# Solving only the diagonal blocks of 16 by substitution, and putting in the corner by two more matmul passes

## The chip, the cores and the metric

One core of a Trainium2 chip runs the kernel. It has a matmul engine (PE, TensorE), a vector engine (DVE), a scalar engine (ACT), GpSimd (POOL) and SyncE (SP), which issues DMAs. The metric is the device time of one execution in microseconds, the median of three runs.

## The reference

The kernel computes one "macaron" layer on x of 8 x 256 x 128: half a feed-forward part (FFN), an attention part, half the same FFN again. The FFN has ternary weights, a gated up projection and two hidden layers of 512. The attention part projects to q, k, v with short causal convolutions, and mixes five paths for each head (4 heads of 32): three FIR filters of v (3, 15 and 64 taps), v itself, and a delta rule by chunks of 32 tokens. A gate computed from x and from statistics of the five paths (mean, mean square, mean absolute value, norm) weighs them.

What the change touches is the delta rule. For each of 8 x 4 x 8 = 256 chunks:

```
attn = where(strict, -(kb @ k^T), 0)     # strictly lower, 32 x 32
T = inv(eye(32) - attn)                  # unit lower triangular
u = T @ v ;  w = T @ kb                  # both 32 x 32
# then over the 8 chunks of a sequence, one after the other:
local = where(incl, q @ k^T, 0)
u_i = u - w @ S ;  o = q @ S + local @ u_i ;  S = S + k^T @ u_i
```

## The kernel before

**Queues and order.** The five engines run their own instruction streams. All of them walk the same list, STEPS, written out by hand in `ffn_steps` and `att_steps`; each step is a kind, a part (0 and 1 the FFNs, 2 the attention) and an index. Engines wait for each other through semaphores, and each engine runs its own steps in the order of the list. PE writes to two rings of four PSUM banks: ring a is emptied by ACT, ring d by DVE; a step takes its banks by its position in the list. SP's queue has the loads of the FIR tiles and of the second FFN's weights, each behind a wait for a PE step.

**Layout.** The 8 sequences are handled in two halves of 4. Within a half, the 128 partitions are 4 sequences x 32 tokens of a chunk (or 4 heads x 32 channels), and for each head and chunk there is a 32 x 32 matrix in each partition block. Matmuls of the delta rule are 32 x 32 weights against 64 columns, four side by side on the array. An fp32 matmul has two records in the trace, and each has a weight load (PEld) beside it.

**The steps of the attention part**, in the order before:

- `qkv`, `sumsq`, `window`: projections with convolutions, norms, transposed windows of v for the FIR.
- `gram` (L851 on PE, L579 on ACT, L1172 on DVE): the products of k with kb and q, masked into `alt`, slot 0 the strict part (-attn), slot 1 the inclusive part.
- `lmat` (L1181): one DVE transpose puts the strict part (L) into the layout of the substitution: one chunk's matrix to a partition, its 32 x 32 elements along the free dimension; half 0's 128 matrices fill the 128 partitions.
- `solve` and, between the masks of the second gram, `substitute` (L1063 to L1074): for each column j of 31, `prod = L[j+1:, j] * T[j, 0:j+1]` and `T[j+1:, 0:j+1] -= prod`, two DVE instructions that depend on each other. Half 1's runs on GpSimd (L459, L461), after half 0's is done.
- `xt` (L1196): DVE transposes the inverse back, as weights for PE.
- `token` (L848): transposes of k, vb and kb to tokens in partitions. `fir` (L872): 16 FIR steps, in FIR_ORDER, the first eight for half 0; each needs its filter tile `toep`, of which two of four groups fit, so that groups are loaded again behind the steps that used them last (L390 to L392).
- `yy` (L884): `T @ [v, kb]`, 8 steps of 64 records. `aq` and `bo` (L894): products of w and u with k and q, 56 and 64 records a step. `first`, `rec`: the recurrence over chunks, a product on PE (L906), an addition (L1220) and a transpose (L1224) on DVE for each of 7 steps and half. `turn3`, `turn4`: the paths into the mixing layout.
- `sq`, `r1`, `r2`, `r3`: the statistics of the 10 path halves; a square on ACT (L502) and three DVE reduces (L1238, L1240, L1244). `turn`: their transpose for the gate.
- `gate` (L915, L917), `logit` (L924), `lturn`, `soft`, `prob`, `mul`, `addmix`, `add`, `rms`, `scale`, `wo`: gate, softmax, mixing, norm and output projection. Those of the first half are put between the steps of the second half's recurrence, those of the second half into the second FFN.

In the order before, half 0's substitution runs while PE does the tokens of both halves, the last eight windows and eight FIR steps. Then come yy, aq and bo of half 0, the recurrence of half 0 with four FIR steps and statistics beside it, yy, gates 0 and 1, aq, logits and bo of half 1, and the recurrence of half 1 with the mixing of half 0.

Of the kernel before, what the change touches and what calls it, by code (L numbers as in the profile page):

```python
# [24 lines left out]
SPLIT = 4  # L25
# [43 lines left out]
def att_steps():  # L69

    s = []
    for t in range(2):
# [23 lines left out]
    s += sums(9)
# [7 lines left out]
          "yy": 1, "bo": 1, "gate": 2, "logit": 1, "addmix": 1}  # L104
RING_D = {"mean": 1, "var": 1, "up": KT, "down": 1, "sumsq": 2, "gram": H, "aq": 1, "rec": 1,
# [30 lines left out]
STATS = ((4, 0), (0, 0), (1, 0), (2, 0), (4, 1), (3, 0), (0, 1), (1, 1), (2, 1), (3, 1))  # L136
# [10 lines left out]
         mtau=47, rt0=55, epsd=48)  # L147
# [6 lines left out]
          vk=0, bo=0, yu=4096, lmat0=32768, tinv0=33792, lmat1=6144, tinv1=7168, ssb=22016, alt=8192, vt0=24576, vt1=16384, aq1=19968, xt=14336, paths=24576,  # L154
          sq=36864, st=34816, stt=4096, hid=6144, hid0=16384, lg=18432, pl=4096, small=12288,
# [3 lines left out]
def program(nc, d, out):  # L159
    ctx = ExitStack()  # L160
    with ctx:
# [60 lines left out]
        sb("paths1", [128, AO["st"] - AO["paths"]], F32, c3)  # L222
# [15 lines left out]
        def ln_bufs(f):  # L238
            if f == 1:
# [124 lines left out]
        def _(e):  # L364
# [940 lines left out]
```

## Time and profile before

| what | us |
|---|---|
| median of three runs | 440.77 |
| lowest, highest | 439.73, 440.98 |
| profiled execution | 442.02 |
| its span | 440.3 |

The attention part takes the stretch from about 130 to 325 us. Every number in the rows further down is read from this one profiled execution. A row of a timeline merges like instructions that follow each other; "idle before" is the time in which the engine had nothing running, with what ended it, and "issue" there means that nothing in the profile accounts for it.

### The profile page before, as it was taken

How to read it: one execution, taken by the hardware profiler on the slowest of the kernel's cores; microseconds unless marked ns; L12 is line 12 of the kernel's file. 1: busy time of each engine (PE TensorE's matmuls, PEld its weight loads, DVE VectorE, ACT ScalarE, POOL GpSimd, SP SyncE). 2: the span in 40 equal slices, each digit the busy share in tenths (PEclk: the TensorE clock that was granted, in tenths of full speed). 3: DMA queues.
4: the chain of work that ended last, by engine and by line, in shares of the span. 5: the costliest groups of instructions: out<-in, count | busy, mean ns of one | idle time of the engine just before them, and what ended most of it. 6: DMA issues, size and time to landing. Idle time of an engine off the chain costs nothing.

```text
span 440.3 us, 9783 instructions
## 1 busy us (share of the span) xinstructions
PE 371.1 (84%) x4132; PEld 278.6 (63%) x4132; DVE 294.8 (67%) x461; ACT 277.7 (63%) x434; POOL 41.9 (10%) x103
## 2 busy tenths in 40 slices
PE   5599999999999998899488489366599687978996
PEld 3377776678866876799377376233267465556885
DVE  2796679628216845699696968667868696578433
ACT  4788956879677776383243265451576838558973
POOL 4000000000000100000788400000000000000000
PEclk9899999999999996889956889585999898989999
DMA  8900007400000000071600001600000000001001
GB/s 272 333 1 2 2 0 227 111 1 1 1 1 0 0 2 3 4 214 49 173 5 4 1 4 36 230 1 1 0 1 3 1 0 2 0 1 49 3 1 48
DMA packets 14325, 19.75 MB, mean 45 GB/s; under 512 B 960, under 2 KB 9152, under 8 KB 14272
## 3 DMA queue, kind: packets, MB, share of 16 engines
q1 hardware_dynamic: 14128, 18.94, 14.4%
q8 instruction: 44, 0.72, 0.6%
q14 instruction: 9, 0.07, 0.1%
q10 hardware_dynamic: 144, 0.01, 0.0%
HBM read 17.91 MB, written 1.05 MB: 43 GB/s over the span
## 4 chain that ended last, share of the span: by engine, by line
PE 58%; DVE 26%; issue 7%; ACT 7%; DMA 1%; DVEq 0%; SPq 0%; ACTq 0%
PE ps_a L723 11%; PE ps_a L724 11%; PE ps_a L827 8%; PE ps_a L894 2%; PE ps_a L884 2%; DVE arena L1074 2%; DVE arena L1071 2%; PE ps_d L794 2%; PE ps_d L858 2%; PE ps_a L917 2%; DVE acts L1121 2%; PE ps_d L724 2%; PE ps_d L723 2%; PE ps_d L894 2%; DVE hbuf L1116 2%
## 5 line engine op out<-in xcount | busy, mean ns | idle before, releaser
L723 PE MATMUL ps_a<-acts,w_f 128*128 128x512 f32 x256 | 103.6, 405 | 9.1 <-ACT acts L597 8.5
L724 PE MATMUL ps_a<-acts,w_f 128*128 128x512 f32 x256 | 101.7, 397 | 0.0
L723 PEld LDWEIGHTS ps_a<-acts,w_f 128*128 128x128 f32 x256 | 49.2, 192 | 22.6 <-ACT acts L597 10.2
L724 PEld LDWEIGHTS ps_a<-acts,w_f 128*128 128x128 f32 x256 | 49.2, 192 | 10.9 <-issue 0.7
L597 ACT ACTIVATE acts<-ps_a,vec 128x512 fp32r<-128x512 f32 x64 | 44.6, 697 | 0.0
L827 PE MATMUL ps_a<-xnp,conv_w 128*128 128x512 f32 x156 | 38.5, 404 | 0.0
L1140 DVE TENSOR_TENSOR acts<-gbuf,acts 128x512 fp32r<-128x512 f32 x32 | 21.6, 689 | 24.9 <-ACT acts L597 24.9
L1140 DVE TENSOR_TENSOR acts<-ghbuf,acts 128x512 fp32r<-128x512 f32 x32 | 21.2, 689 | 20.8 <-ACT acts L597 20.8
L827 PEld LDWEIGHTS ps_a<-xnp,conv_w 128*128 128x128 f32 x156 | 29.3, 188 | 8.2 <-issue 1.4
L987 DVE SCALAR_TENSOR_TENSOR arena<-ps_d,arena 128x512 f32<-128x512 f32 x16 | 11.0, 686 | 30.4 <-ACT arena L551 26.3
L594 ACT ACTIVATE gbuf<-ps_a,vec 128x512 f32<-128x512 f32 x32 | 22.3, 697 | 10.3 <-PE ps_a L724 10.2
L594 ACT ACTIVATE ghbuf<-ps_a,vec 128x512 f32<-128x512 f32 x32 | 22.4, 699 | 7.2 <-PE ps_a L724 7.1
L872 PE MATMUL ps_a<-toep,arena 96*32 96x96 f32 x512 | 23.8, 356 | 0.0
L906 PE MATMUL ps_d<-arena 32*32 32x64 f32 x448 | 11.6, 256 | 13.3 <-issue 6.7
L872 PEld LDWEIGHTS ps_a<-toep,arena 96*32 96x32 f32 x512 | 20.1, 130 | 3.1 <-issue 1.6
L723 PE MATMUL ps_a<-xn,w_f 128*128 128x512 f32 x32 | 15.3, 477 | 7.7 <-DVE ln L988 5.1
L906 PEld LDWEIGHTS ps_d<-arena 32*32 32x32 f32 x448 | 9.0, 129 | 19.2 <-issue 10.7
L502 ACT ACTIVATE arena<-arena 128x1024 f32<-128x1024 f32 x10 | 10.3, 1050 | 16.6 <-DVE arena L1227 16.3
L459 POOL TENSOR_TENSOR arena<-arena 128x31 f32<-128x31 f32 (+15 forms) x31 | 15.6, 503 | 46.9 <-DVE arena L1196 44.6
L642 ACT ACTIVATE arena<-ps_a 128x384 f32<-128x384 f32 x16 | 7.9, 491 | 17.1 <-PE ps_a L872 17.0
L884 PE MATMUL ps_a<-arena 32*32 32x64 f32 x512 | 10.2, 243 | 9.9 <-DVE arena L1196 5.3
L1116 DVE SCALAR_TENSOR_TENSOR hbuf<-ps_d,vec,gbuf 128x512 f32<-128x512 f32 x16 | 11.6, 748 | 8.4 <-ACT gbuf L567 5.2
(211 smaller groups left out, 778.5 us busy)
## 6 DMA issues: line engine op xcount, KB each, us to landing
toep<-in_fir SPq DMA_DIRECT2D x24, 288.0 KB, 6.5
w_in<-in_h SPq DMA_DIRECT2D x4, 1024.0 KB, 8.2
g_rows<-in_gW SPq DMA_DIRECT2D x4, 640.0 KB, 6.7
w_in<-in_w SPq DMA_DIRECT2D x6, 256.0 KB, 4.7
iobuf<-in_x SPq DMA_DIRECT2D x4, 256.0 KB, 6.5
toep<-in_taps SPq DMA_DIRECT2D x1, 768.0 KB, 6.7
y<-iobuf SPq DMA_DIRECT2D x3, 256.0 KB, 2.4
toep<-in_proj SPq DMA_DIRECT2D x1, 256.0 KB, 8.6
```

What stands on the lines that cost most here:

```text
L459: own(e.tensor_tensor(prod, lmat[1][:, j + 1:DH, j:j + 1].to_broadcast(shape), tinv[1][:, j:j + 1, 0:j + 1].to_broadcast(shape), ALU.mult))
L594: e.activation(gbuf[f][:, gi % 4], src[:, :], ACT.Gelu, scale=sc).then_inc(S["act_step"], 1)
L597: e.activation(acts[f][:, j % 3, 0, m], src[:, :], ACT.Gelu, scale=sc).then_inc(S["act_a"], 1)
L723: e.matmul(bank, w, hi, start=start, stop=False)
L724: return e.matmul(bank, w, lo, start=False, stop=stop)
L827: last = e.matmul(bank, conv_w[:, hw, ww], xnp[:, hx, 2 * i:2 * i + 2, o:o + L], start=n == 0, stop=n == len(todo) - 1)
L872: last = e.matmul(bank[32 * h:32 * h + 32, WIN * c4:WIN * c4 + WIN], vt[half][0:WIN, DH * h + 8 * grp + dl, :], toep[0:WIN, grp % 2, h, :, ...
L884: last = e.matmul(bank[r, 64 * n:64 * n + 64], xt[r, g, h, n], vk[r, g, h, n].rearrange("p x c -> p (x c)"), start=True, stop=True)
L894: last = e.matmul(bank[c, 64 * n:64 * n + 64], yu[r, g, h, n, o:o + DH], alt[g][r, h, n, 1:3].rearrange("p x c -> p (x c)"), start=True, s ...
L906: last = e.matmul(bank[r, 64 * b:64 * b + 64].rearrange("p (x t) -> p x t", x=2), s_sb[r, g, b], aqs[g][r, b, n], start=True, stop=True)
L1116: e.scalar_tensor_tensor(out=hbuf[f][:, m % 2], in0=ps_d[:, (dd + m) % NRING], scalar=vc("s2", m), in1=gbuf[f][:, (KT * j + m) % 4], op0=A ...
L1140: e.tensor_tensor(acts[f][:, j % 3, 1, m], gbuf[f][:, (KT * j + m) % 4], acts[f][:, j % 3, 0, m].bitcast(F32), ALU.subtract).then_inc(S["d ...
```

## The change

The unit lower matrix I - attn is split into its two diagonal blocks of 16 and the lower left 16 x 16 corner, called N here. The inverse D of the two diagonal blocks is found by substitution, for both blocks in one instruction, 15 steps instead of 31. The corner is put in by three passes on PE instead of one:

- `zz`: y = D [v, kb], evicted by ACT with a scale of 1 for the upper 16 tokens of a chunk and 0 for the lower (`top`);
- `ww`: N y, made with slot 0 of `alt`, where GpSimd has set the diagonal blocks' columns to zero (semaphore `cut`); DVE subtracts it from [v, kb] in place;
- `yy`: D ([v, kb] - N y), as before.

zz and ww have 8 steps each, of 64 records, as yy. GpSimd does half 1's blocks instead of the whole matrices, and begins when half 1's `lmat` is there. The steps are put in a new order. These are its core lines:

```
-    s += fir[0:4] + [("gram", 2, 1), ("lmat", 2, 1), ("solve", 2, 2), ("xt", 2, 0)]
-    s += [("token", 2, i) for i in (0, 1, 4, 5, 8, 9, 2, 3, 6, 7, 10, 11)]
-    s += [("window", 2, i) for i in range(8, 16)] + fir[4:12]
-    s += [("yy", 2, k) for k in range(4)] + [("turn4", 2, 0), ("turn4", 2, 1), ("sq", 2, 0), ("sq", 2, 1)] + sums(0)
...
+    s += fir[0:4] + [("solve", 2, 1), ("gram", 2, 1), ("lmat", 2, 1)]
+    s += [("token", 2, i) for i in (0, 1, 4, 5, 8, 9)] + [("zz", 2, k) for k in range(4)]
+    s += [("turn4", 2, 0)] + [("ww", 2, k) for k in range(4)] + [("turn4", 2, 1), ("r1", 2, 0), ("numbers", 2, 0)]
+    s += [("yy", 2, k) for k in range(4)] + [("token", 2, 10), ("token", 2, 11), ("r2", 2, 0)]
+    s += [("aq", 2, k) for k in range(4)] + [("bo", 2, k) for k in range(4)] + [("first", 2, 0)]
+    beside = {1: [("token", 2, 2), ("token", 2, 3)], 2: [("token", 2, 6), ("token", 2, 7), ("xt", 2, 1)],
+              3: [("window", 2, i) for i in range(8, 12)], 4: [("window", 2, i) for i in range(12, 16)] + [("sq", 2, 0)],
+              5: [fir[4], ("r3", 2, 0)], 6: [fir[5], ("sq", 2, 1), ("r1", 2, 1)], 7: [fir[6], ("r2", 2, 1)]}
     for n in range(1, NCH):
         s += [("rec", 2, n)] + beside[n]
+    s += [("turn3", 2, 0), fir[7], ("sq", 2, 2), ("r3", 2, 1)] + [("zz", 2, k) for k in range(4, 8)] + sums(2)
+    s += [("sq", 2, 3), ("ww", 2, 4), ("ww", 2, 5), ("ww", 2, 6), ("ww", 2, 7)] + [("yy", 2, k) for k in range(4, 8)] + sums(3)
+    s += [("sq", 2, 4)] + fir[8:10] + sums(4) + [("sq", 2, 5)] + [("bo", 2, k) for k in range(4, 8)] + sums(5) + fir[10:16]
+    s += [("turn", 2, 0)] + [("aq", 2, k) for k in range(4, 8)]
     half = [None] + [("rec", 2, NCH + n) for n in range(1, NCH)]
+    s += [("first", 2, 1), ("gate", 2, 0), ("sq", 2, 6), half[1], ("gate", 2, 1), ("r1", 2, 6), half[2], ("sq", 2, 7), ("r2", 2, 6),
+          ("logit", 2, 0), ("r3", 2, 6), half[3], ("logit", 2, 1)] + sums(7) + [("sq", 2, 8), ("lturn", 2, 0), ("soft", 2, 0)]
+    s += [half[4], ("round", 2, 0), ("r1", 2, 8), ("prob", 2, 0), ("mul", 2, 0), half[5], ("mul", 2, 1), ("addmix", 2, 0),
+          ("add", 2, 1), ("osq", 2, 1), half[6], ("r2", 2, 8), ("rms", 2, 0), half[7], ("r3", 2, 8), ("scale", 2, 0),
+          ("turn3", 2, 1), ("wo", 2, 0), ("wo", 2, 1), ("sq", 2, 9)] + sums(9)
```

The substitution, the new steps on PE, ACT and DVE, and GpSimd's part:

```
+SOLVED = (4, 6, 9, 12, HB - 1)
+STATS = ((4, 0), (4, 1), (0, 0), (1, 0), (2, 0), (3, 0), (0, 1), (1, 1), (2, 1), (3, 1))
             def substitute(first, last):
                 for j in range(first, last):
+                    k = HB - 1 - j
+                    shape = [128, 2, k, j + 1]
+                    sub = tblk[0][:, :, j + 1:HB, 0:j + 1]
...
                 elif kind == "gram":      # DVE
                     for h in range(H):
+                        if i and h == H - 1:
+                            turn_inverse(0)
...
+                        if i and h < H - 1:
+                            substitute(SOLVED[h + 1], SOLVED[h + 2])
...
+                elif kind == "ww":        # PE
+                    e.wait_ge(S["cut"], g + 1)
+                    e.wait_ge(S["act_a"], A_AT[("zz", 2, i)] + 1)
...
+                            last = e.matmul(bank[r, 64 * n:64 * n + 64], alt[g][r, h, n, 0], yu[r, g, h, n],
+                                            start=True, stop=True)
...
+                    if kind == "zz":
+                        e.wait_ge(S["inv_done"], g + 1)
+                        e.wait_ge(S["act_a"], A_AT[("token", 2, (9, 7)[g])] + 1)
+                    else:
+                        e.wait_ge(S["dve_d"], D_AT[("ww", 2, i)] + 1)
...
+                elif kind == "ww":        # DVE
+                    v = vk[:, i // 4, i % 4].rearrange("p n x c -> p (n x c)")
+                    e.wait_ge(S["pe_d"], dd + 1)
+                    e.tensor_tensor(v, v, ps_d[:, dd % NRING], ALU.subtract).then_inc(S["dve_d"], 1)
...
+                elif kind == "zz":        # ACT
+                    e.activation(yu[:, i // 4, i % 4].rearrange("p n c -> p (n c)"), bank[:, :], ACT.Identity,
+                                 scale=vc("top")).then_inc(S["act_a"], 1)
...
-            e.wait_ge(S["inv_done"], 1)   # GpSimd
-            for j in range(DH - 1):
+            e.memset(alt[0][:, :, :, 0, 0:HB], 0.0).then_inc(S["cut"], 1)
+            own(e.memset(st[0][:, :, 4 * P:32], 0.0))
+            e.wait_ge(S["l_turned"], 2)
+            for j in range(HB - 1):
```

Buffers move in the shared arena to make room (aq has one buffer for both halves, the statistics one for each half). GpSimd makes `top` with five small memsets before it signals the masks. SP's load of the second FFN's weights now waits for the last FIR step instead of logit 1:

```
-            e.wait_ge(S["pe_a"], A_AT[("logit", 2, 1)] + 1)
+            e.wait_ge(S["pe_a"], A_AT[("fir", 2, FIR_ORDER[15])] + 1)
```

The loads of the FIR tiles keep their conditions: group 0 is loaded again after FIR step 11 (the tenth in FIR_ORDER), group 1 after step 15 (the twelfth); they are used by steps 2, 3 (13th, 14th) and 6, 7 (15th, 16th).

## Rows read from the trace of the kernel before

**Rows 1.** The page: each engine's busy us, share of the span, instructions.

```profile
PE 371.1 (84%) x4132; PEld 278.6 (63%) x4132; DVE 294.8 (67%) x461; ACT 277.7 (63%) x434; POOL 41.9 (10%) x103
```

**Rows 2.** Chain of waits around 210 us: start us, us, what.

```profile
208.04 2.02 DVE arena L1196
...
210.11 1.98 PE ps_a L884 x125
```

**Rows 3.** PE's timeline, 186 to 209 us: start us, us, instruction, count.

```profile
186.38 7.83 PE L848 MATMUL ps_a<-ident,arena 128*128 128x128 f32 x48
...
194.04 3.73 PE L845 MATMUL ps_a<-ident,arena 128*96 128x128 f32 x32
...
197.71 11.49 PE L872 MATMUL ps_a<-toep,arena 96*32 96x96 f32 x256
```

**Rows 4.** DVE's timeline, steps of the substitution of half 0, 112 elements.

```profile
174.56 0.28 DVE L1074 TENSOR_TENSOR arena<-arena 128x112 f32<-128x112 f32 x1
```

**Rows 5.** PE's timeline, small matmuls (in brackets: idle before, releaser).

```profile
164.37 2.95 PE L858 MATMUL ps_d<-arena 32*32 32x64 f32 x224
...
168.76 1.08 PE L858 MATMUL ps_d<-arena 32*32 32x64 f32 x32 [1.44 <-issue]
...
218.76 0.42 PE L884 MATMUL ps_a<-arena 32*32 32x64 f32 x4 [3.24 <-issue]
...
230.63 2.60 PE L894 MATMUL ps_a<-arena 32*32 32x64 f32 x103 [1.19 <-issue]
...
234.33 1.08 PE L906 MATMUL ps_d<-arena 32*32 32x64 f32 x32 [1.11 <-issue]
...
252.03 5.70 PE L884 MATMUL ps_a<-arena 32*32 32x64 f32 x256 [4.40 <-DVE arena L1196]
...
267.32 1.76 PE L894 MATMUL ps_d<-arena 32*32 32x64 f32 x112
...
277.27 2.11 PE L894 MATMUL ps_a<-arena 32*32 32x64 f32 x80 [2.13 <-issue]
```

**Rows 6.** Timeline of the other engines at the edges of the steps.

```profile
213.47 0.46 POOL L459 TENSOR_TENSOR arena<-arena 128x135 f32<-128x135 f32 x1
...
187.92 1.95 DVE L1181 STREAM_TRANSPOSE arena<-arena 128x1024 f32<-128x1024 f32 x1
...
190.09 0.60 ACT L635 ACTIVATE arena<-ps_a 128x512 f32<-128x512 f32 x1 [0.26 <-PE ps_a L848]
...
233.92 0.31 DVE L1215 STREAM_TRANSPOSE arena<-arena 128x128 f32<-128x128 f32 x1 [1.65 <-ACT arena L650]
...
248.26 1.90 DVE L1227 STREAM_TRANSPOSE arena<-arena 128x1024 f32<-128x1024 f32 x1
...
281.81 2.83 DVE L1028 TENSOR_TENSOR arena<-arena 128x2560 f32<-128x2560 f32 x1
...
313.10 1.21 DVE L1244 TENSOR_REDUCE arena<-arena 128x32 f32<-128x1024 f32 x1
```

**Rows 7.** SyncE's DMA issues, then stretches: length, busy us, PE clock, DMA share, GB/s.

```profile
206.41 5.91 SPq L359 DMA_DIRECT2D toep<-in_fir  x8
...
208.00:210.00 2.00, 1.20 (x28) 0.80 (x20) 1.97 (x2) 0.81 (x2) 0.00 (x0) 1.00 1.04 301
...
216.00:218.00 2.00, 0.00 (x0) 0.00 (x0) 0.09 (x1) 0.00 (x0) 1.76 (x4) 1.00 0.16 50
```

**Rows 8.** DVE by line, 139 to 327 us: busy us, mean ns.

```profile
L1240 DVE TENSOR_REDUCE arena<-arena 128x32 f32<-128x1024 f32 x10 | 12.2, 1219 | 0.0
...
L1220 DVE TENSOR_TENSOR arena<-arena,ps_d 128x256 f32<-128x256 f32 (+1 forms) x14 | 5.6, 398 | 7.9 <-PE ps_d L906 7.9
...
L1224 DVE STREAM_TRANSPOSE arena<-arena 128x128 f32<-128x128 f32 x12 | 3.7, 311 | 0.4
...
L1000 DVE TENSOR_TENSOR x_t<-x_t,ps_d 128x512 f32<-128x512 f32 x2 | 1.4, 689 | 2.3 <-PE ps_d L764 2.3
```

**Rows 9.** PE's timeline, first product of the gates.

```profile
260.94 0.95 PE L915 MATMUL ps_a<-xnp,gate_x 128*128 128x512 f32 x3 [0.34 <-DVE arena L1250]
```

More of the change, by code:

```diff
@@ L24 @@
 NRING = 4
-SPLIT = 4
+SOLVED = (4, 6, 9, 12, HB - 1)
 def ffn_steps(f):
@@ L103 @@
 RING_A = {"in": 1, "flag": 1, "gsum": 1, "up": KT, "hid1": KT, "hid2": KT, "out": 1, "qkv": 4, "window": 1, "token": 1, "fir": 1,
-          "yy": 1, "bo": 1, "gate": 2, "logit": 1, "addmix": 1}
-RING_D = {"mean": 1, "var": 1, "up": KT, "down": 1, "sumsq": 2, "gram": H, "aq": 1, "rec": 1,
+          "zz": 1, "yy": 1, "bo": 1, "gate": 2, "logit": 1, "addmix": 1}
+RING_D = {"mean": 1, "var": 1, "up": KT, "down": 1, "sumsq": 2, "gram": H, "ww": 1, "aq": 1, "rec": 1,
           "wo": 1}
@@ L146 @@
          atau=28, gbt=28, etau=29, eeps=30, lntau=35, s3h=36, itau=37, eps=38, rest=43, l2eps=44, lneps=45, rmseps=46,
-         mtau=47, rt0=55, epsd=48)
+         mtau=47, rt0=55, epsd=48, top=27)
 NVEC = 27
@@ L221, in program @@
         fin = sb("fin", [128, 2, TILE], F32, c3)
-        sb("paths1", [128, AO["st"] - AO["paths"]], F32, c3)
+        sb("paths1", [128, AO["vpad"] - AO["paths"]], F32, c3)
         xn_1 = sb("xn1", [128, 2, 2, TILE], F32R, c3)
@@ L279, in program @@
                  "pe_a act_a pe_d dve_d dve_lo act_hi act_sq act_t dve_xn xn_pad pad_zero "
-                 "act_ss act_nt dve_nrm eye_done l_turned pool_inv inv_done path4 state act_l nums summed act_osq "
+                 "act_ss act_nt dve_nrm eye_done l_turned cut pool_inv inv_done path4 state act_l nums summed act_osq "
                  "st_zero act_stat dve_stat act_norm path3 st_turned ld_h2 act_exp dve_sub mixed dve_ms act_rms "
@@ L433, in _ @@
             own(e.tensor_copy(pick[:, 16:20], head_w[:, 0:128:32]))
+            own(e.memset(vc("top"), 0.0))
+            for q in range(4):
+                own(e.memset(vec[32 * q:32 * q + HB, V["top"]:V["top"] + 1], 1.0))
             e.tensor_scalar(pick[:, 16:19], pick[:, 16:19], 1.0 / DH, None, ALU.mult).then_inc(S["mask_done"], 1)
@@ L501, in squares @@
                     e.wait_ge(S["path3"], g + 1)
-                e.activation(sq_p[:, q % 2], paths[p][:, g], ACT.Square).then_inc(S["act_stat"], 1)
+                if p < 3:
+                    e.wait_ge(S["act_a"], A_AT[("fir", 2, FIR_ORDER[8 * g + 7])] + 1)
+                e.activation(sq_p[:, (q + 1) % 2], paths[p][:, g], ACT.Square).then_inc(S["act_stat"], 1)
             def preload(table):
@@ L875, in _ @@
                     last.then_inc(S["pe_a"], 1)
-                elif kind == "yy":
+                elif kind == "ww":
                     g, h = i // 4, i % 4
-                    e.wait_ge(S["inv_done"], g + 1)
-                    e.wait_ge(S["act_a"], A_AT[("token", 2, 11)] + 1)
+                    e.wait_ge(S["cut"], g + 1)
+                    e.wait_ge(S["act_a"], A_AT[("zz", 2, i)] + 1)
+                    bank = take_d(dd)
+                    for n in range(NCH):
+                        for b in range(4):
+                            r = slice(32 * b, 32 * b + 32)
+                            last = e.matmul(bank[r, 64 * n:64 * n + 64], alt[g][r, h, n, 0], yu[r, g, h, n],
+                                            start=True, stop=True)
+                    last.then_inc(S["pe_d"], 1)
+                elif kind in ("zz", "yy"):
+                    g, h = i // 4, i % 4
+                    if kind == "zz":
[3 more added lines that the diff above has]
+                        e.wait_ge(S["dve_d"], D_AT[("ww", 2, i)] + 1)
                     bank = take_a(a)
@@ L905, in _ @@
                             r = slice(32 * h, 32 * h + 32)
-                            last = e.matmul(bank[r, 64 * b:64 * b + 64].rearrange("p (x t) -> p x t", x=2), s_sb[r, g, b],
-                                            aqs[g][r, b, n], start=True, stop=True)
+                            last = e.matmul(bank[r, 64 * b:64 * b + 64].rearrange("p (x t) -> p x t", x=2), s_sb[g][r, b],
+                                            aqs[r, b, n], start=True, stop=True)
                     last.then_inc(S["pe_d"], 1)
@@ L1214, in _ @@
                     e.wait_ge(S["act_a"], A_AT[("bo", 2, 4 * i + 3)] + 1)
-                    e.transpose(s_sb[:, i].rearrange("p b c -> p (b c)"), bo[:, i, 0, :, 1]).then_inc(S["state"], 1)
+                    e.transpose(s_sb[i].rearrange("p b c -> p (b c)"), bo[:, i, 0, :, 1]).then_inc(S["state"], 1)
                 elif kind == "rec":
@@ L1223, in _ @@
                         e.wait_ge(S["dve_d"], dd + 1)
-                        e.transpose(s_sb[:, g].rearrange("p b c -> p (b c)"), bo[:, g, n, :, 1]).then_inc(S["state"], 1)
+                        e.transpose(s_sb[g].rearrange("p b c -> p (b c)"), bo[:, g, n, :, 1]).then_inc(S["state"], 1)
                 elif kind == "turn3":
```

101 lines of the change are left out of this document (41 added, 60 removed).

## Prediction

> **What bounds the kernel now.** I read the page's engine line first, then the chain of waits from 130 to 330 us, then each engine's timeline from 160 to 330 us. PE has most work (371.1 us of 440.3), DVE 294.8, POOL 41.9 [rows 1]. The change touches only the attention part. There the chain runs down DVE's substitution for half 0, into its transpose at 208.04 and from there into PE's first products with the inverse at 210.11 [rows 2]: at first sight the substitution, some 20 us of serial DVE steps, is the bound. PE's timeline says otherwise. From 186.38 to 209.20 PE transposes tokens (7.83 us), windows (3.73 us) and runs eight FIR steps (11.49 us) without a gap [rows 3]. It waited 0.9 us for the inverse. So the substitution hides 22.8 us of PE work that must be done anyway; a quicker inverse gains only what the new order finds to put beside other waits.
>
> The second thing to see is how PE runs its small matmuls (32x32 weights, 64 columns). 224 records take 2.95 us, and then PE stands 1.44 us with nothing to wait for but "issue" [rows 5]. Such gaps come after each 125 to 128 records of a train: the trains that begin at 218.76 and 230.63 stand behind gaps of 3.24 and 1.19 us [rows 5]. From 218.76 to the end of the train at 233.23 there are 4 records of the last inverse product and 480 of aq and bo, 484 or 3.8 blocks of 127, in 14.5 us: 3.8 us a block, 29.9 ns a record. A train that begins after slow work finds two blocks ready: 4.4 us from 164.37 to the third at 168.76 [rows 5]. Without gaps a record takes 22.3 ns (5.70 us for 256, at 252.03) or 15.7 ns (1.76 us for 112, at 267.32) [rows 5]. I read the gaps as the supply of instructions, two for each record (weight load and matmul).
>
> **The change, part by part.**
>
> *Substitution.* Half 0 had 31 steps of two DVE instructions; it has 15 on two blocks at once, of 30 to 128 elements. A step with 112 elements took 0.28 us an instruction [rows 4]; with the 0.04 us between two, 30 instructions by some 0.29 are 8.7 us against 23.2 before. Bounds for the new access pattern: 0.20 to 0.43 us, the shortest and longest instruction of the old one. DVE's order in the second gram: after the first mask at 182.3 come three steps (2.0), a mask (0.4), three (1.8), a mask, three (1.5), the inverse's transpose (1.95, as the transpose at 187.92 [rows 6]): it ends near 191. The sixth token's eviction ends at 190.09 + 2 x 0.86 + 0.60 = 192.4 [rows 6] and so ends last. The first pass (zz) starts at 192.5 instead of 210.1: 17.6 us earlier. At 0.43 us an instruction it would be 195.
>
> *Half 1 on GpSimd.* 30 instructions, 0.46 us at 135 elements with 0.08 between [rows 6], so at most 16 us from 193.4, done by 209. Its transpose stands in the second recurrence step, past 228: 19 us of cover, no cost. The memsets that cut out the corner wait for transposes long past. Five small memsets ahead of the masks lie in the first 30 us, where the masks aren't wanted: nothing.
>
> *Two more passes.* zz and ww are 8 steps each of 64 records, as yy: 1024 new records. Sum at the rates above: 30 us at 29.9 ns, 16 at 15.7. On ACT, zz adds 8 evictions by 0.60 [rows 6]; on DVE, ww adds 8 subtractions of 512 columns by 0.69 [rows 8], so DVE ends up 14.5 - 5.5 = 9 us lighter. Both trail PE one step behind and show only at the end of a pass. yy has a new wait, for the subtraction of its own step: ahead of the four subtractions DVE has one transpose (1.9 us, from 193.4), done before ww begins; behind them wait a transpose and reduces that nobody needs soon. ww waits for the cut and for zz's eviction, and behind it on PE is everything, yet both are there a pass ahead.
>
> *Half 0 up to its first state.* zz, ww, yy (768 records), two tokens (8), aq (224), bo (256): 1256 records or 9.9 blocks; two in 4.4 us, 7.8 by 3.8, together 34.0. From 192.5 that is 226.5, and with an eviction and its latency `first` is at 227.5; it was at 233.9 [rows 6]. So of the 17.6 us, 6.4 are left.
>
> *Recurrence of half 0.* It took 14.0 us, from 234.3 to 248.3 [rows 5, 6], with four FIR steps beside it. Now four tokens, eight windows and three FIR steps lie beside it, and DVE has its second inverse transpose in step 2 (1.95). A step with windows has PE at 0.65 + 1.9; I take 15.0 us: it ends at 242.5, PE at 242.
>
> *From there to the last aq of half 1*, PE's own queue: one FIR step 1.4, an eighth of 11.49 [rows 3]; zz, ww, yy 768 records or 6.1 blocks, 4.4 + 4.1 x 3.8 = 19.8; two FIR 2.9; bo 256 records, two blocks 7.6, less 1 for what the FIR steps let through, 6.6; four FIR 5.8; two more 2.9; aq, 224 records, 4.4. That is 43.8. Two things come on top. The filter tiles: the load of the last group is issued when FIR step 15 is done, and it is used two FIR steps (2.9 us) later. Before, eight loads were issued from 206.41, the DMA engines were full at 208 and had all but ended at 216 [rows 7]: about 4.2 us a group, 5.5 to 6.5 with the start. PE waits some 3.5 us; before, this load had 20 us of cover. And the load of the group before it lies across bo: such loads stood beside the 3.24 us gap [rows 5], so 1.7 more. PE is done with aq at 242 + 49 = 291 (I call this T). DVE has, in the same 49 us, 26 us of work: one turn of paths (1.9), 13 reduces (15.6), four subtractions, a transpose (2), eight aq halves (3.2). It stands idle for some 20 us, and can't go ahead, since ACT's square roots for its `turn` stand behind the last FIR evictions and the recurrence behind aq.
>
> *Tail.* Before, PE ended bo at 279.4 [rows 5] and DVE the last sum of half 0's mixing and half 1's statistics at 314.3 [rows 6]; sums 6 to 8 and both gates had been done before. Now they come behind T. DVE's work: 12 reduces 14.6, seven adds and transposes of the recurrence 5.0 [rows 8]; three large transposes 5.8; two products 5.6 [rows 6]; adds 2.6, scale 1.8, rms 1.4, probabilities 1.5, softmax 0.7, two additions of wo 1.4: 40.4 us. Ahead of it stand 1.1 us for the last aq and `first`, and the first gate (two steps took 260.94 to 267.32, so 3.2 each [rows 5, 9]), behind which step 8 is queued on PE. With 0.5 for the rest it is 45: 336.0 against 314.3, and from there both kernels do the same. The weights for the second FFN are now requested at T - 4.5 and wanted at T + 19: hidden, as 11 us sufficed before.
>
> *Sum.* -17.6 (start of the passes), +11.2 (to `first`: 35.0 us against 23.8), +0.6 (to the end of the recurrence), +27.5 (from there to the last reduce: 93.5 us against 66.0, PE's queue and the tail) make +21.7 us. The profiled execution took 442.02 (span 440.3), 1.25 above the median of the runs, 440.77. So 442.0 + 21.7 - 1.25 = 462.5; I say 462.
>
> On the supply of instructions the traces show gaps of 1.2 to 3.2 us after some 127 records [rows 5]. The Trainium skill, "Runtime: NRT & Kernel Launch", section "Instruction fetch mechanics", says that engines stream their instructions in blocks of 256 and that this is hidden by the pace of issue. The block size agrees with the spacing; that it is hidden does not. By that rule the time would be rival A's or B's.
>
> **Rivals.**
> A. *The supply keeps up, the clock stays at its lower level*: records at 22.3 ns without gaps. 1256 records take 28.0 (-6.0), and 1248 of half 1 take 27.8 (-3.4 against 31.2): +12.3, 453. For it: 252.03, 256 records without a gap, but these came after 4.4 us of rest. Against it: every longer train has gaps.
> B. *The other sign: supply without gaps and PE at 2.4 GHz.* 15.7 ns a record: 19.7 us (-14.3) and 19.6 (-11.6), and 4 us less in recurrence, FIR and gates: -8.2, 432.5. Since -17.6 is gained before the first product, it decides at about 18.5 ns a record: below it the kernel gets faster. For it: PE has no long rests in the new order, and 224 records did run at 13.2 ns (164.37) [rows 5]. Against it: the train at 252.03 ran at 22.3 ns without any gap, and after each long gap the records are slower (230.63: 103 in 2.60) [rows 5].
> C. *Everything collides*: FIR, tokens and gates at the lower clock after each gap (some 30 steps by 0.2 = 6 us), filter loads that hold up two blocks of instructions instead of one (3), a tail with 3 us of more waits: +34, 474.
> D. *DVE sets the end throughout.* From 193.4 it has 23 + 26 + 40 us of work and the 17 us of waits that it had before: 300, -14, 427. It needs PE's 2500 records to vanish behind DVE; PE's queue above speaks against it.
>
> **How the numbers follow.** Forecast 0.50, A 0.23, C 0.13, B 0.08, D 0.03, no change 0.03. Within 0.3% (1.3 us) a measurement of this kernel can't tell a change. Faster is B, D and a little of the lower edge of A: 0.11; same 0.03; slower 0.86. The range goes from between A and B, 444, to C, 474. The likeliest case alone spans 456 to 468.
>
> **What would show it.** The first product with the inverse near 192.5; records of the three passes at 25 ns or more with "issue" gaps each 127; `first` of half 0 near 227; PE waiting for the filter tiles before FIR steps 6 and 7; DVE idle for some 20 us between 245 and 290; the last reduces near 336. It would be wrong if the trains run without gaps at 16 ns, or if DVE has no such idle stretch.

## The result, and the profile after

| | before | changed |
|---|---|---|
| median, us | 440.88 (4 runs) | 479.76 (4 runs) |
| lowest, highest | 439.73, 441.45 | 475.45, 480.81 |
| profiled execution's span | 440.3 | 477.8 |

The changed kernel is slower: ratio 1.087, 95% interval 1.080 to 1.094. The direction was forecast, and most of the mechanisms; the size was not: 462 was said, with 474 as the upper end.

The page after: PE has 21.7 us more of busy time and 1024 more instructions, DVE 8.2 us less, GpSimd half of what it had [rows 1].

```profile
PE 392.8 (82%) x5156; PEld 298.2 (62%) x5156; DVE 286.6 (60%) x437; ACT 283.6 (59%) x442; POOL 21.9 (5%) x79
```

PE's timeline, half 0's passes. The inverse no longer sets their start; a train of 184 records starts at 191.62, then the gaps begin:

```profile
191.62 2.77 PE L915 MATMUL ps_a<-arena 32*32 32x64 f32 x184 [0.79 <-issue]
197.82 2.14 PE L915 MATMUL ps_a<-arena 32*32 32x64 f32 x72 [3.43 <-issue]
...
201.62 3.02 PE L901 MATMUL ps_d<-arena 32*32 32x64 f32 x127 [0.17 <-issue]
205.70 1.24 PE L901 MATMUL ps_d<-arena 32*32 32x64 f32 x73 [1.06 <-issue]
...
209.41 2.02 PE L915 MATMUL ps_a<-arena 32*32 32x64 f32 x127 [1.69 <-issue]
213.40 1.75 PE L915 MATMUL ps_a<-arena 32*32 32x64 f32 x76 [1.97 <-issue]
```

The same for half 1. Here the engine ran quickly (127 records in 2.0 us) and still the pieces start 4.0 us apart; what the records don't use is idle time with the label "issue":

```profile
248.07 2.66 PE L915 MATMUL ps_a<-arena 32*32 32x64 f32 x176
252.14 1.32 PE L915 MATMUL ps_a<-arena 32*32 32x64 f32 x80 [1.41 <-issue]
...
256.12 1.99 PE L901 MATMUL ps_d<-arena 32*32 32x64 f32 x127 [2.00 <-issue]
260.11 1.33 PE L901 MATMUL ps_d<-arena 32*32 32x64 f32 x81 [2.00 <-issue]
...
264.09 2.59 PE L915 MATMUL ps_a<-arena 32*32 32x64 f32 x127 [2.00 <-issue]
267.80 2.56 PE L915 MATMUL ps_a<-arena 32*32 32x64 f32 x84 [1.12 <-issue]
```

The trace shows what ends these gaps. The profile counts a DMA queue named "instruction" beside the data queues (packets, MB, share of the 16 engines); the first row is the kernel before, the second the changed one:

```profile
q8 instruction: 44, 0.72, 0.6%
q8 instruction: 52, 0.85, 0.8%
```

All its packets have 16,384 bytes, and 8 more packets for 2048 more instructions on PE (1024 matmul records, 1024 weight loads) are one for 256. A piece of 127 records with its weight loads has 254. In half 1's passes each packet starts 1.1 to 1.5 us after a piece and takes 1.2 to 1.4 us, and the next piece starts 1.3 to 1.5 us after the packet's end. The last three rows are packets beside data transfers; there the packet starts late (3.45 and 3.15 us after the piece) or takes longer (2.24 us). All times are from the trace of the changed kernel:

| piece starts | instruction packet, start to end | next piece starts |
|---|---|---|
| 252.14 | 253.63 to 254.85 | 256.12 |
| 256.12 | 257.36 to 258.77 | 260.11 |
| 260.11 | 261.29 to 262.61 | 264.09 |
| 264.09 | 265.23 to 266.39 | 267.80 |
| 191.62 (184 records) | 195.07 to 196.25 | 197.82 |
| 275.91 | 279.06 to 280.13 | 281.63 |
| 296.08 (166 records) | 297.26 to 299.50 | 300.95 |

By this order of events a gap labelled "issue" here is a wait for instructions, as the prediction had read it. No run changed the queue itself.

Then the rest of PE's queue up to the last aq (compare the end of bo at 277.27 + 2.11 in [rows 5]). The third row waits for DMA, the last for "issue":

```profile
275.91 2.92 PE L925 MATMUL ps_a<-arena 32*32 32x64 f32 x127 [1.04 <-issue]
281.63 0.86 PE L925 MATMUL ps_a<-arena 32*32 32x64 f32 x23 [2.81 <-issue]
...
293.12 3.03 PE L889 MATMUL ps_a<-toep,arena 96*32 96x96 f32 x64 [4.84 <-DMA toep<-in_fir]
...
300.95 1.84 PE L925 MATMUL ps_d<-arena 32*32 32x64 f32 x58 [2.54 <-issue]
```

DVE's timeline at the edges of the stages: the inverse's transpose (187.76), `first` of half 0 (229.93; before 233.92), the end of its recurrence (245.27; before 248.26), the turn that waits 20.61 us for ACT, and the last reduce (350.59; before 313.10) [rows 6].

```profile
187.76 1.97 DVE L1110 STREAM_TRANSPOSE arena<-arena 128x1024 f32<-128x1024 f32 x1
...
229.93 0.31 DVE L1249 STREAM_TRANSPOSE arena<-arena 128x128 f32<-128x128 f32 x1 [7.33 <-ACT arena L667]
...
245.27 0.29 DVE L1254 TENSOR_TENSOR arena<-arena,ps_d 128x128 f32<-128x128 f32 x1
```

```profile
297.18 1.97 DVE L1284 STREAM_TRANSPOSE arena<-arena 128x1024 f32<-128x1024 f32 x1 [20.61 <-ACT arena L675]
...
350.59 1.21 DVE L1278 TENSOR_REDUCE arena<-arena 128x32 f32<-128x1024 f32 x1
```

By stages (length; busy us of PE, PEld, DVE, ACT, GpSimd; granted clock, DMA share, GB/s): in the third stage, 58 us, DVE worked for 24.9 us. In the fourth it worked for 38.4 of 49.

```profile
245.00:303.00 58.00, 38.24 (x1585) 34.41 (x1574) 24.92 (x29) 20.46 (x33) 0.00 (x0) 0.79 0.22 64
303.00:352.00 49.00, 31.06 (x274) 14.79 (x274) 38.37 (x50) 20.96 (x25) 0.00 (x0) 0.76 0.10 36
```

### The profile page after: what moved, and what is told of

Its sections match the earlier page's. It is cut to its first block, busy times and chain, and to the rows that moved or that the text cites. A ratio compares the mean times of both kernels' runs of the same rounds, so it can differ in the third digit from the quotient of the medians.

```text
span 477.8 us, 11817 instructions
## 1 busy us (share of the span) xinstructions
PE 392.8 (82%) x5156; PEld 298.2 (62%) x5156; DVE 286.6 (60%) x437; ACT 283.6 (59%) x442; POOL 21.9 (5%) x79
## 4 chain that ended last, share of the span: by engine, by line
PE 36%; DVE 14%; issue 8%; ACT 4%; DMA 1%; SPq 0%; DVEq 0%; ACTq 0%
PE ps_a L740 4%; PE ps_a L741 4%; PE ps_a L915 4%; PE ps_a L889 3%; PE ps_a L925 2%; PE ps_a L865 2%; PE ps_d L901 2%; PE ps_a L948 2%; PE ps_d L925 2%; PE ps_a L946 2%; PE ps_a L961 2%; DVE hbuf L1151 1%; PE ps_d L937 1%; DMA toep<-in_fir 1%; DVE arena L1061 1%
## 5 line engine op out<-in xcount | busy, mean ns | idle before, releaser
L740 PEld LDWEIGHTS ps_a<-acts,w_f 128*128 128x128 f32 x256 | 49.7, 194 | 21.9 <-ACT acts L609 10.2
L741 PEld LDWEIGHTS ps_a<-acts,w_f 128*128 128x128 f32 x256 | 49.7, 194 | 11.0 <-issue 0.7
L1175 DVE TENSOR_TENSOR acts<-gbuf,acts 128x512 fp32r<-128x512 f32 x32 | 21.7, 688 | 25.6 <-ACT acts L609 25.6
L915 PE MATMUL ps_a<-arena 32*32 32x64 f32 x1024 | 19.6, 236 | 12.4 <-issue 12.4
L606 ACT ACTIVATE gbuf<-ps_a,vec 128x512 f32<-128x512 f32 x32 | 22.3, 695 | 11.0 <-PE ps_a L741 10.9
L606 ACT ACTIVATE ghbuf<-ps_a,vec 128x512 f32<-128x512 f32 x32 | 22.3, 698 | 7.3 <-PE ps_a L741 7.2
L915 PEld LDWEIGHTS ps_a<-arena 32*32 32x32 f32 x1024 | 17.9, 119 | 14.0 <-issue 14.0
L889 PEld LDWEIGHTS ps_a<-toep,arena 96*32 96x32 f32 x512 | 19.8, 136 | 8.3 <-DMA toep<-in_fir 5.2
L663 ACT ACTIVATE arena<-ps_a 128x512 f32<-128x512 f32 x8 | 4.8, 597 | 26.1 <-PE ps_a L915 26.1
L1284 DVE STREAM_TRANSPOSE arena<-arena 128x1024 f32<-128x1024 f32 x2 | 3.9, 1945 | 21.2 <-ACT arena L675 21.2
L937 PE MATMUL ps_d<-arena 32*32 32x64 f32 x448 | 10.4, 237 | 7.4 <-DVE arena L1258 6.3
L925 PE MATMUL ps_a<-arena 32*32 32x64 f32 x512 | 12.1, 289 | 5.2 <-issue 5.2
```

The costliest lines, as they stand in the source:

```text
L606: e.activation(gbuf[f][:, gi % 4], src[:, :], ACT.Gelu, scale=sc).then_inc(S["act_step"], 1)
L740: e.matmul(bank, w, hi, start=start, stop=False)
L741: return e.matmul(bank, w, lo, start=False, stop=stop)
L889: last = e.matmul(bank[32 * h:32 * h + 32, WIN * c4:WIN * c4 + WIN], vt[half][0:WIN, DH * h + 8 * grp + dl, :], toep[0:WIN, grp % 2, h, :, ...
L915: last = e.matmul(bank[r, 64 * n:64 * n + 64], xt[r, g, h, n], vk[r, g, h, n].rearrange("p x c -> p (x c)"), start=True, stop=True)
L925: last = e.matmul(bank[c, 64 * n:64 * n + 64], yu[r, g, h, n, o:o + DH], alt[g][r, h, n, 1:3].rearrange("p x c -> p (x c)"), start=True, s ...
```

## The experiments

Differences from the changed kernel are taken through each run's ratio to the kernel before, times 441 us. By the two intervals such a difference is uncertain by 3.5 to 4 us. Four kernels leave the corner of the inverses out and only price the work: "Without the passes", "The block substitution alone", "No passes, no late tiles", and the last one for half 0. "Half the columns" leaves out half of what zz and ww compute.

### Without the passes

```
-STEPS = ffn_steps(0) + att_steps() + ffn_steps(1)
+STEPS = [s for s in ffn_steps(0) + att_steps() + ffn_steps(1) if s[0] not in ("zz", "ww")]
-                    if kind == "zz":      # PE: wait for the inverse and the tokens
+                    if kind == "yy":
```

> The changed kernel with its new order, but without the steps zz and ww: only yy is left, so the corner of each inverse is left out. 1024 records and the two evictions and subtractions a step go. Theory S (PE is supplied with instructions at one block of some 127 matmul records in 4.0 us, whatever the clock, as the starts behind the gaps of the changed kernel at 252.1, 256.1, 260.1, 264.1 and 267.8 us say): 8.06 blocks by 4.0 = 32 us less, 447.5. Rival R (only the execution of the records costs, 16 to 23 ns each): 16 to 23 us less, 457 to 463. Rival O (the new order costs the time, the passes lie beside DVE's work): less than 10 us, 470 or more.

Measured 447.01, ratio 1.013 (1.009 to 1.016): 32.7 us less than the changed kernel. Theory S had 32; R and O are out for the size. The two added passes are five sixths of the loss of 38.9. The instruction queue is back at 44 packets.

### The passes alone, in the order before

```
+    if _s[0] == "yy" and _s[2] % 4 == 0:
+        STEPS += [("y2", 2, _s[2] + k) for k in range(4)] + [("y3", 2, _s[2] + k) for k in range(4)]
-                elif kind == "yy":        # PE and ACT
+                elif kind in ("y2", "y3", "yy"):
```

> The kernel before with each yy step done three times into the same place (redundant work, same result): 1024 records and 16 evictions more, order and substitution as before. Theory S: +32 us, 473. Rival R: +16 to +23, 457 to 464. Rival O: the passes find cover in the order before, less than +10, under 451.

Measured 471.73, ratio 1.068 (1.062 to 1.074): +30 us, 29 ns for each of the 1024 records, between S and R and nearer to S. So the passes cost the same in either order, within the intervals. The pieces of the second train start 3.4 to 4.0 us apart:

```profile
265.85 6.30 PE L888 MATMUL ps_a<-arena 32*32 32x64 f32 x301 [4.41 <-DVE arena L1200]
273.54 1.99 PE L888 MATMUL ps_a<-arena 32*32 32x64 f32 x127 [1.40 <-issue]
277.53 1.98 PE L888 MATMUL ps_a<-arena 32*32 32x64 f32 x127 [2.00 <-issue]
280.96 1.99 PE L888 MATMUL ps_a<-arena 32*32 32x64 f32 x127 [1.46 <-issue]
284.67 1.42 PE L888 MATMUL ps_a<-arena 32*32 32x64 f32 x86 [1.72 <-issue]
```

### Half the columns, the same instructions

```
-    e.matmul(bank[r, 64 * n:64 * n + 64], alt[g][r, h, n, 0], yu[r, g, h, n], ...)
+    e.matmul(bank[r, 64 * n:64 * n + 32], alt[g][r, h, n, 0], yu[r, g, h, n, 0:32], ...)
     # zz likewise: columns 0 to 31 of [v, kb]
```

> The changed kernel with zz and ww on 32 of their 64 columns (the corner of w is left out and its operand is stale): the same number of instructions, half the columns to stream in 1024 records. Theory S: no change, 479.8 within 2 us, the gaps longer by what the records get shorter. Rival R: the records of both passes get shorter by a third or more, -5 us or more, 475 or less.

Measured 476.03, ratio 1.079 (1.075 to 1.083): -3.6 us, no more than the uncertainty of the difference. By the time alone this lies between the two theories. The trace parts them:

```profile
203.10 1.97 PE L901 MATMUL ps_d<-arena 32*32 32x32 f32 x127 [1.47 <-issue]
207.08 1.22 PE L901 MATMUL ps_d<-arena 32*32 32x32 f32 x73 [2.00 <-issue]
...
256.18 1.93 PE L901 MATMUL ps_d<-arena 32*32 32x32 f32 x127 [1.57 <-issue]
260.16 1.33 PE L901 MATMUL ps_d<-arena 32*32 32x32 f32 x82 [2.05 <-issue]
```

Pieces of 127 records with half the columns start 3.98 us apart at 203.10 and 207.08 and at 256.18 and 260.16, as those of the changed kernel at 256.12 and 260.11. Over all of half 1's passes the spacing was 3.4 to 4.0 us, where the changed kernel had 3.7 to 4.0; but the run with the tile load moved, further down, has all its columns and 3.7 us there. Half 0's three passes took 23.4 us with half the columns in two of them and 23.5 with all. Half 1's took 19.7 against 22.2, but 20.1 in that run with all columns. So the columns are worth 0.4 us at most in these traces, and the -3.6 us can't be put down to them.

Nor does the duration of the records set the pace: in the changed kernel 127 of them took 3.02 us at 201.62, 1.99 at 256.12 and 2.59 at 264.09, and the next piece began 4.08, 3.99 and 3.71 us after the start of each. Nor does the clock: the granted clock was 1.00 at 256.1 to 258.1 in the changed kernel and 0.50 at 256.2 to 258.1 in this run. In this run too the piece at 260.16 starts 1.42 us after the end of an instruction packet (257.79 to 258.74).

### The block substitution alone, in the order before

```
-                    k = DH - 1 - j
-                    shape = [128, k, j + 1]
+                    k = HB - 1 - j
+                    shape = [128, 2, k, j + 1]      # and so on, on GpSimd too; no zz, ww
```

> The kernel before, its order kept, with the substitution only inside the diagonal blocks of 16 on DVE and GpSimd and the corner left out: DVE has 14.5 us less to do ahead of the first product with the inverse. My reading of the trace before (PE works without a gap from 186.4 to 209.2 beside the substitution): only the 0.9 us for which PE waits, and at most 2 more from a freed DVE, 437.5 to 440. The rival that the chain of waits suggests (the substitution is the bound): -12 to -14.5, 427 to 429.

Measured 441.23, ratio 0.998 (0.996 to 1.001): -0.7 us, no difference. DVE's transpose of the inverse starts 15 us earlier (193.06 against 208.04 [rows 2]):

```profile
193.06 2.00 DVE L1198 STREAM_TRANSPOSE arena<-arena 128x1024 f32<-128x1024 f32 x1
195.10 4.12 DVE L1202 STREAM_TRANSPOSE arena<-arena 128x1024 f32<-128x1024 f32 x2
```

and PE goes on with tokens, windows and FIR steps until 208.36, without any wait ahead of its first product with the inverse:

```profile
196.92 11.51 PE L874 MATMUL ps_a<-toep,arena 96*32 96x96 f32 x256
208.36 1.98 PE L886 MATMUL ps_a<-arena 32*32 32x64 f32 x125
211.89 2.10 PE L886 MATMUL ps_a<-arena 32*32 32x64 f32 x127 [1.56 <-issue]
217.51 0.42 PE L886 MATMUL ps_a<-arena 32*32 32x64 f32 x4 [3.51 <-issue]
```

The chain of waits named the substitution, but an equally long piece of PE work stood beside it. What the change removed was worth nothing in the old order: 0.7 us, with an interval from 2.0 less to 0.6 more.

### The load of the filter tiles

```
-    s += [("sq", 2, 4)] + fir[8:10] + sums(4) + [("sq", 2, 5)] + [("bo", 2, k) for k in range(4, 8)] + sums(5) + fir[10:16]
+    s += [("sq", 2, 4)] + fir[8:12] + sums(4) + [("sq", 2, 5)] + [("bo", 2, k) for k in range(4, 8)] + sums(5) + fir[12:16]
```

> The changed kernel with the 11th and 12th FIR step moved ahead of bo of half 1, so that the load of the last group of filter tiles is issued some 9 us earlier. Expected by the trace of the changed kernel (PE waits 4.84 us for that load, at 288.3 to 293.1): -4.5 to -5, 475. Rival: the load then lies across bo and holds up instruction blocks there (a gap beside such a load was 2.81 us against 1.0 to 2.0 without one): -2 to -3, 477.

Measured 471.50, ratio 1.070 (1.064 to 1.076): -7.6 us, with an uncertainty of 4; the wait that it removes is 4.84. In its trace FIR steps 13 to 16 run without a wait, and the last aq ends at 295.8 instead of 302.8:

```profile
283.49 5.85 PE L889 MATMUL ps_a<-toep,arena 96*32 96x96 f32 x128
289.27 2.33 PE L925 MATMUL ps_d<-arena 32*32 32x64 f32 x166
293.92 1.84 PE L925 MATMUL ps_d<-arena 32*32 32x64 f32 x58 [2.33 <-issue]
```

The gap in bo grew from 2.81 to 3.82 us (at 281.39), so the collision that the rival named is there, at 1 us. The 7.0 us by which this trace is ahead at the last aq have two parts. From the end of half 1's passes on it is 5.3 us quicker: the wait, and 0.5. The other 2.1 us lie ahead of the move, in half 1's passes, which took 20.1 us instead of 22.2: their pieces start 3.71 us apart (3.7 to 4.0 in the changed kernel), and the last records ran at the higher clock (granted 1.00 from 267.2 on, against 0.50 from 267.8 on). The order of these steps is the same in both kernels, and the run with the recurrence early has 20.3 us there. What makes the pace differ from trace to trace is open.

### The recurrence of half 1 earlier

```
+    s += [("aq", 2, k) for k in range(4, 8)] + [("turn", 2, 0)]
+    s += [("first", 2, 1), ("gate", 2, 0), half[1], ("gate", 2, 1), half[2], ("logit", 2, 0), fir[10], half[3], ("logit", 2, 1), fir[11],
+          half[4], ("lturn", 2, 0), ("soft", 2, 0), fir[12], fir[13], half[5], ("prob", 2, 0), ("mul", 2, 0), fir[14], fir[15],
+          half[6], ("sq", 2, 6), ("mul", 2, 1), ("addmix", 2, 0), half[7], ...   # then sums 6 to 9
```

> The changed kernel (all its passes) with aq, turn and first of half 1 right behind bo, and the last six FIR steps, both gates and logits beside the recurrence of half 1; sums 6 to 8 come behind them. PE's work is the same, but DVE no longer stands 20.6 us for the turn that ACT holds back behind the FIR evictions. Theory O2 (the place of these steps in the order costs 15 us or more, since the work behind them is DVE's): -15 to -20, 460 to 465. Rival (PE's queue with its supply sets the end however the steps stand): less than -8, 472 or more.

Measured 476.15, ratio 1.079 (1.074 to 1.084): -3.4 us, no more than the uncertainty. The forecast of theory O2 falls. The recurrence does start 13 us earlier (the first step at 294.64 instead of 307.70), and it keeps that: its last addition is at 322.39 instead of 339.06. But DVE waited 18.3 us for PE in it, in six waits, against 8.6 in three, and had no reduces to put there, since those of sums 6 to 8 need the last FIR steps. The last tile load costs another 2.64 us on PE:

```profile
294.64 0.65 PE L939 MATMUL ps_d<-arena 32*32 32x64 f32 x32
...
313.37 2.99 PE L891 MATMUL ps_a<-toep,arena 96*32 96x96 f32 x64 [2.64 <-DMA toep<-in_fir]
```

```profile
295.35 0.42 DVE L1256 TENSOR_TENSOR arena<-arena,ps_d 128x256 f32<-128x256 f32 x1 [5.56 <-PE ps_d L939]
...
299.23 0.42 DVE L1256 TENSOR_TENSOR arena<-arena,ps_d 128x256 f32<-128x256 f32 x1 [3.11 <-PE ps_d L939]
...
303.24 0.42 DVE L1256 TENSOR_TENSOR arena<-arena,ps_d 128x256 f32<-128x256 f32 x1 [3.24 <-PE ps_d L939]
...
322.39 0.29 DVE L1256 TENSOR_TENSOR arena<-arena,ps_d 128x128 f32<-128x128 f32 x1 [1.59 <-PE ps_d L939]
...
347.35 1.22 DVE L1280 TENSOR_REDUCE arena<-arena 128x32 f32<-128x1024 f32 x1
```

So 12 reduces of the statistics stand behind the recurrence, 4 in the changed kernel; the last one ends at 348.57 instead of 351.80. Of the 16.7 us gained at the end of the recurrence 3.2 are left. DVE's 20 idle us were not a gap that this order could fill: the move closed them and opened others. That no order can fill them isn't shown.

### Half 1 by GpSimd's whole inverse

```
-            for j in range(HB - 1):       # GpSimd, blocks
+            for j in range(DH - 1):       # whole, as before
-    [("zz", 2, k) for k in range(4, 8)] ... ("ww", 2, 4), ("ww", 2, 5), ("ww", 2, 6), ("ww", 2, 7)
```

> The changed kernel, in which half 1 has no second and third pass: GpSimd finds its whole inverse in 31 steps, which took 36.5 us in the kernel before, from 193 on, so until 230; the inverse's transpose stands near 235. 512 records less on PE. Theory S: 4.03 blocks by 4.0 = 16 us less, 464; GpSimd's longer work costs nothing. Rival: GpSimd ends late, or slows DVE beside it: 466 to 470.

Measured 462.06, ratio 1.048 (1.043 to 1.053): -17.2 us for 512 records. S had 16. The instruction queue has 48 packets, 4 less. GpSimd's 31 steps stayed off the path (done at 228.6, the transpose that needs them starts at 235.03), so for half 1 the passes bought nothing.

### Both of these

The diff is the two above together.

> The two before together: half 1 by GpSimd's whole inverse without extra passes, and the recurrence of half 1 ahead of the last FIR steps, gates beside it. Candidate for a version that beats both kernels. If the two gains add: 479.8 - 16 - 17 = 447. If DVE becomes the bound in between they overlap: 450 to 455. Below 440 only if the freed order gives more than the trace shows.

Measured 462.26, ratio 1.050 (1.045 to 1.054): the same as with GpSimd alone. Both forecasts, 447 and 450 to 455, missed: the earlier recurrence adds nothing. As above, no reduce of sums 6 to 9 stands beside it (its last step is at 307.64, and the reduces start at 308.56).

### No passes, no late tiles

The diffs of the first and the fifth experiment together.

> The new order with neither the extra passes (the corner of the inverses is left out) nor the late load of filter tiles (11th and 12th FIR step ahead of bo). If the two causes add, 447.0 - 8.3 = 438.7: the whole loss is then these two, and the inverse that comes 17 us earlier gains nothing but a balance with the longer tail. Rival (they overlap, since a shorter train leaves the tile load later in relation to it): 442 to 445.

Measured 443.75, ratio 1.002 (0.998 to 1.007): no difference from the kernel before. The plain sum, 438.7, lies outside of the interval (440.6 to 444.5); the rival's 442 to 445 holds. The late tiles are worth 4.5 us here (1.0126 to 1.0023) and 7.6 with the passes, a difference that the intervals don't resolve. With both causes gone the whole loss is gone, and an inverse that stands 15 us earlier, with an order made for it, has earned nothing.

### A different order for the second half

```
+    s += [("sq", 2, 4)] + fir[8:12] + sums(4) + [("sq", 2, 5)] + [bo 4 to 7] + sums(5) + [("turn", 2, 0)]
+    s += fir[12:16] + [("gate", 2, 0), ("sq", 2, 6), ("gate", 2, 1)] + sums(6) + [("sq", 2, 7)] + [aq 4 to 7]
+    s += sums(7) + [("sq", 2, 8), ("first", 2, 1), ("logit", 2, 0), ("logit", 2, 1), half[1], ...
```

> Half 1 by GpSimd's whole inverse (no passes of its own), the 11th and 12th FIR step ahead of bo, turn of half 0 ahead of the last four FIR steps, and the gates and sums 6 and 7 ahead of the recurrence of half 1. From 462.1 (GpSimd alone): 7 us for the tiles, and 3 to 8 for DVE's sums ahead of the recurrence: 446 to 452. The rival by the run with the recurrence early (-3.6 only): nothing more than the tiles, 455. If it is below 441 it beats both kernels.

Measured 460.10, ratio 1.041 (1.034 to 1.048), 3 us below GpSimd's whole inverse alone, and the two intervals overlap: nothing more than part of the tiles' gain. It ends above the forecast range of 446 to 452, and above the rival's 455. Its twin without the passes of half 0:

> The same without the passes of half 0 too (the corner of half 0's inverses is left out; half 1's are whole). Theory S: 512 records or 16 us less than the kernel beside it. It shows what a free block inverse of half 0 would be worth in an order made for it: 430 to 436 if supply and DVE leave room, 440 if not.

Measured 456.53, ratio 1.034 (1.026 to 1.041): only 3.2 us below the kernel beside it, where S said 16, and far from 430 to 440. Most of the reason is in DVE's timeline. Without the passes `first` of half 0 is 13.4 us earlier than in the kernel beside it (216.53 against 229.90), and the transpose of half 1's inverse in the second recurrence step meets GpSimd before it is done (229.9 us):

```profile
216.53 0.31 DVE L1247 STREAM_TRANSPOSE arena<-arena 128x128 f32<-128x128 f32 x1 [6.81 <-ACT arena L665]
...
230.05 1.90 DVE L1108 STREAM_TRANSPOSE arena<-arena 128x1024 f32<-128x1024 f32 x1 [8.28 <-POOL vec L470]
...
233.75 0.42 DVE L1252 TENSOR_TENSOR arena<-arena,ps_d 128x256 f32<-128x256 f32 x1 [1.20 <-PE ps_d L935]
```

DVE stands 8.28 us, the recurrence behind it, and at the last step of half 0's recurrence only 4.7 us of the 13.4 are left (240.70 against 245.37 on PE). The passes had been the cover of GpSimd's 31 steps: a wait that the trace with the passes doesn't show. No version tried beats the kernel before.

## Why the prediction was wrong

Its own milestones against the trace (us from the span's start):

| step | forecast | measured | stage, forecast | stage, measured |
|---|---|---|---|---|
| first product with the inverse | 192.5 | 191.6 | | |
| `first` of half 0 | 227.5 | 229.9 | 35.0 | 38.3 |
| end of recurrence, half 0 | 242.5 | 245.6 | 15.0 | 15.6 |
| PE done with the last aq | 291 | 302.8 | 49 | 57.7 (from 245.1) |
| last reduce | 336.0 | 351.8 | 45 | 49.0 |
| against before | +21.7 | +37.5 | | |

*Right:* the bound. PE's work hid the substitution. The block substitution alone changed nothing, and the new order gained 18.5 us at the first product and kept 4.0 at `first` (6.4 forecast). GpSimd's half cost nothing in the change itself. ACT and DVE trailed the passes. DVE's idle stretch came, from 276.6 to 297.2, for the reason named (ACT's square roots behind the FIR evictions). The tile load was late, by 4.84 us (3.5 forecast).

*Wrong: the step "From there to the last aq of half 1", PE's own queue, by 8.7 us (57.7 against 49), and within it the head start of a train.* I took two blocks, 254 records, in 4.4 us at the start of each train, and 3.8 us for each other one. The second figure was near: 3.7 to 4.1. The first was not. The second train's first gap came after 176 records, and its second piece began after 4.07 us. The three passes took 22.2 us against 19.8. At the forecast 29.9 ns a record the other 592 records would have taken 17.7 us, so about 2.0 of the 2.4 us are the head start; the rest is the pace, which was quicker in other traces (20.1 us for these passes with the tile load moved, 20.3 with the recurrence early). That "two blocks are ready" came from one row (164.37); the trains here had 184, 176 and 169 records before their first gap. The same row was used for aq, 6.7 us against 4.4, with the second FFN's weights arriving beside it (a gap of 2.54 us); I had priced the collision of a load with bo but not this one. bo took 9.2 us against 8.3, the tile wait 1.3 more than forecast. And 1.5 us is a FIR step that I had counted beside the last recurrence step, while PE does it after that step: 2.4 + 2.3 + 0.9 + 1.3 + 1.5 = 8.4 of the 8.7.

*Too small, too: the way to `first`, by 3.3 us,* for the same reason, and here nearly all of it: the three passes took 23.5 us against 19.8. The first 184 records and the gap of 3.43 us behind them took 6.2 us, the other 584 ran at 29.6 ns each. The gap, at 194.4, stands beside the tile loads issued from 186.06 on (rows of the kernel before showed 3.24 beside such loads; I had used it only for half 1). Two slips in the prediction's sums are small: 7.9 blocks by 3.8 and 4.4 are 34.4 and not 34.0, and 4.4 + 4.1 x 3.8 is 20.0 and not 19.8.

*And the tail, by 4.0 us.* DVE's work was 38.4 us (40.4 forecast), its waits 10.6 and not 4.6. I priced the first recurrence step behind a gate at 3.2 us, the row of a quick gate; DVE waited 4.66 there and 2.01 at the next. With 0.6 more in the recurrence of half 0, and 0.9 less at the start of the passes, these terms add up to 15.7 of the 15.8 us by which the last reduce came later than forecast.

*The rivals.* A and B needed the gaps to go. They didn't, and pieces of quick records (1.99 us) came no closer to each other than the slow ones. C, at 474, was nearest; of its list the filter loads (a tile wait of 4.84 us and a gap of 2.81) and the longer waits in the tail are in the trace, its price for the lower clock after gaps wasn't tested. I gave it 0.13. Two readings behind the rivals were off: the 22.3 ns taken for the lower clock come from a row with a granted clock of 0.64 (at 0.50, the 127 records at 226.53 of the kernel before took 2.92 us, 23 ns), and the row cited against B (230.63) stands behind a gap of 1.19 us, not behind a long one. The Trainium skill, "Runtime: NRT & Kernel Launch", section "Instruction fetch mechanics", has fetching hidden by the pace of issue: the trace of the changed kernel, with gaps of 0.2 to 3.4 us between the pieces of its passes, each ended by an instruction packet, disagrees.

## What to carry to other kernels

A chain of waits that runs down one engine says nothing of what a shortening is worth until the timeline of the engine at its end is read: if that engine worked without a gap up to the wait, the chain is one of two equals. Price many small matmuls by the number of their instructions (here 26 to 31 ns a record in trains of 768), not by columns or by the duration of a record, and look in the trace whether the idle time between them ends with a packet of the instruction queue. And when a step moves in a hand-written order, list the loads whose trigger and use move with it, and the other engine's work that had been its cover.

## What the runs showed of the hardware

- Trains of 32x32 matmuls with fp32 operands run in pieces of 127 records that start mostly 3.4 to 4.1 us apart, of which the records take 1.9 to 3.6. The spacing is the same with half the columns (3.4 to 4.0) and at a granted clock of 0.50 or 1.00.
- Each piece behind a gap labelled "issue" in these passes starts 1.2 to 1.6 us after the end of a 16,384-byte packet of the instruction queue.
- Behind a piece that runs beside DMA transfers the gap is longer: 3.43 us after the changed kernel's first 184 records (DMA share 1.04 beside them), 2.81 after the piece at 275.91 (0.93), 2.54 after the one at 296.08 (0.44), 5.12 in the half-column run at 199.68 (1.03). The packet then starts late or takes longer, as the table above shows.

```profile
199.68 1.22 PE L916 MATMUL ps_a<-arena 32*32 32x32 f32 x72 [5.12 <-issue]
```

- The substitution's DVE instructions on two blocks at once cost as the old ones of their size (112 elements, 0.28 us [rows 4]): 128 elements 0.29 us, 30 elements 0.19.

```profile
182.71 0.29 DVE L1102 TENSOR_TENSOR arena<-arena 128x128 f32<-128x128 f32 x1
...
187.31 0.19 DVE L1102 TENSOR_TENSOR arena<-arena 128x30 f32<-128x30 f32 x1
```
